# The head of a two-layer mixer kernel: x and base_w landing in turn, and sums taken off TensorE

## The chip, the cores and the metric

One core of one Trainium2 chip. The metric is the device time of one execution of the kernel, in microseconds (us), taken as the median of several runs. The engines are named as in the profile: PE is TensorE, ACT is ScalarE, DVE is VectorE, POOL is GpSimd, SP is the engine whose queue issues most DMAs. PE works on SBUF operands and writes PSUM banks (`ps`, 8 banks of 128 x 512 float32).

## The reference

Two layers, each with a small conditioning part and a mixture-of-experts part, on x of 64 x 32 x 512. Cut to what matters:

```
def _L0_cond_ref(x, embedding, W0, b0, W1, b1, W2, b2, weight, bias_k):
    h = jax.nn.gelu(embedding @ W0 + b0, approximate=False)
    h = jax.nn.gelu(h @ W1 + b1, approximate=False)
    att = jax.nn.softmax((h @ W2 + b2) / T, axis=-1)
    agg_w = jnp.einsum('bk,koi->boi', att, weight[..., 0])
    agg_b = att @ bias_k
    return jnp.einsum('boi,bih->boh', agg_w, x) + agg_b[:, :, None]

def _L0_ffn_ref(x, gate_w, base_w, base_b, lora_A, lora_B):   # E=8, top 2, R=16
    gate_logits = jnp.einsum('bsd,ed->bse', x, gate_w)
    weights, selected = jax.lax.top_k(gate_logits, K)
    weights = jax.nn.softmax(weights, axis=2)
    result = jnp.einsum('bsd,od->bso', x, base_w) + base_b
    w_full = jnp.sum(jax.nn.one_hot(selected, E) * weights[..., None], axis=2)
    low = jnp.einsum('bsd,erd->ebsr', x, lora_A)
    return result + SCALING * jnp.einsum('ebsr,eor,bse->bso', low, lora_B, w_full)

x = x + _L0_ffn_ref(_L0_cond_ref(x, cond_128, ...), ...)
x = x + _L1_ffn_ref(_L1_cond_ref(x, cond_128, ...), ...)
```

`_L1_cond_ref` is a grouped convolution of 9 taps plus a context row per batch, and `_L1_ffn_ref` again a mixture (4 experts, top 2, R=16) without a base product.

## The kernel before, in words

The 2048 rows (64 batches x 32 channels) are cut into G = 4 groups of TG = 4 tiles of 128 rows. The width D = 512 is cut into DC = 4 chunks of 128, and x is held transposed: `xT_s[:, g % 2, c, :]` is chunk c of group g, 128 x 512. Mixing over channels (`agg_w`) commutes with the products over D, so the kernel first multiplies x by the weights and then mixes the small results with `mixT`, a block-diagonal matrix per tile.

Precision: large products are made from parts. A value is split into a high part (float32r, by ACT) and a low part (full minus high, by DVE or POOL), and `hi_lo` (L951 to 958) issues three matmuls: high x high (L955), low x high (L956), high x low (L957).

For group 0 the head does, in PE's program: filler matmuls on a matrix of ones (`keep_busy`, L948); the attention network (L1168 to L1177); the column sums of `lgw` (LoRA A and gate weights together, 136 columns) by a matmul with ones (L1180), which multiply the bias of the mixing; the logits of x by `lgw` in full float32 (`x_logits`, L969, which the compiler splits into two passes); the attention turned and spread over tiles (L1185, L1188); `mixb` and `ctx` (L1193, L1195), which DVE copies out as `mixbias` and `ctxbias`; the product with base_w (`x_base`, into the four PSUM banks `P0`, one per tile); the mixing of the logits (`mix_logits`, L986); the sums of base_w over its inputs (L1209, by ones, and L1217, which turns the row into a column); and the turning of the gated LoRA values (`turn_lw`, L1029). Then comes the first product of group 1 (`x_first(1, t)`, 264 columns, into the same banks `P0`, so it waits for `p0_out(0, t)`, ACT's copy of bank t to SBUF), then `make_y(0)`, four steps of `mix_base` (L1047) and `experts0`, with the bias row (L1058) in the first, then `mix_logits(1)`, the sums for the second layer (L1230), `x_base(1)`, `turn_lw(1)`, the bias row of group 1 and `make_y(1)`. DVE makes `bias_x(i, c)` (x plus bias times the sum of base_w, L717) and `make_x1(i, c)` (L723) from each y; step c >= 2 of `make_y` writes the PSUM bank of step c - 2 and waits for its `make_x1`. From i = 1 on a loop overlaps the second layer of one group with the first layer of a later one.

The order on each engine is the order in which the code is written; semaphores order the engines among each other. All loads go through SP's queue in program order, except `wrep`, which ACT issues. DVE's routing (`route0`) hands `dif` to ACT (`gate_exp`, L465) and takes it back; its result is `lw`. POOL makes the low parts of group 1 (`x_low(1, c)`, tile `xTl`) after `lb_lo`, the low part of LoRA B that DVE makes behind the routing.

## Time and profile before

| | |
|---|---|
| median of 3 runs | 182.52 us (182.43 to 183.62) |
| profiled execution | 182.84 us, of which the span is 181.1 us |
| busy in the span: PE, PE weight load | 174.1 us, 162.4 us |
| busy in the span: DVE, ACT, POOL | 131.9 us, 82.1 us, 84.1 us |
| matmul instructions recorded | 1123 |
| HBM read, written | 7.77 MB, 4.19 MB |

The span runs from the first to the last instruction. Busy times are sums of recorded durations. A matmul's recorded duration includes its way through the array, so that a row of matmuls overlaps; what one costs in a full queue is the distance between starts, which the chain gives.

### The profile page before, as it was taken

The numbers are of one execution on the slowest core, as the hardware profiler recorded it, in microseconds if no ns is written. First come the engines' busy times: TensorE is split into PE (matmuls) and PEld (weight loads), VectorE is DVE, ScalarE is ACT, GpSimd is POOL, SyncE is SP. The second block draws the span as 40 slices with busy tenths as digits, with TensorE's granted clock in tenths as the row PEclk, the third lists the DMA queues.
The fourth block names the chain that finished last, engine by engine and source line by source line (L and its number), as shares of the span: only waits on it lengthen the run. The fifth ranks groups of instructions, "written<-read, shape, count | busy, mean of one in ns | idle before, by whom it ended". The sixth has DMA issues, their size and how long they took to land.

```text
span 181.1 us, 3129 instructions
## 1 busy us (share of the span) xinstructions
PE 174.1 (96%) x1123; PEld 162.4 (90%) x1123; DVE 131.9 (73%) x270; ACT 82.1 (45%) x189; POOL 84.1 (46%) x86
## 2 busy tenths in 40 slices
PE   7999999999999999999999999999999999989990
PEld 7998888988997799999989999999899999988870
DVE  6159999979967943997996436997997943578471
ACT  3657747860635357525143267422315553244021
POOL 7024605992083979950009199630008693434000
PEclk9999999999999999999999999999999999999999
DMA  5999000004200330000033000000131000000336
GB/s 183 304 370 375 25 0 2 0 5 160 72 0 4 125 109 0 4 0 0 2 117 119 0 0 4 0 0 0 43 134 58 2 5 0 0 0 4 116 116 232
DMA packets 6351, 12.16 MB, mean 67 GB/s; under 512 B 704, under 2 KB 1088, under 8 KB 6336
## 3 DMA queue, kind: packets, MB, share of 16 engines
q1 hardware_dynamic: 6192, 11.84, 18.4%
q8 instruction: 9, 0.15, 0.3%
q10 hardware_dynamic: 144, 0.13, 0.3%
q14 instruction: 6, 0.05, 0.1%
HBM read 7.77 MB, written 4.19 MB: 66 GB/s over the span
## 4 chain that ended last, share of the span: by engine, by line
PE 90%; DVE 6%; issue 1%; ACT 0%; POOL 0%; DVEq 0%; POOLq 0%
PE ps L955 22%; PE ps L957 22%; PE ps L956 22%; PE ps L1047 7%; PE ps L948 3%; PE ps L969 2%; PE ps L986 2%; PE ps L1148 2%; PE ps L1149 2%; PE ps L1029 1%; PE ps L1180 1%; PE ps L1209 1%; PE ps L1058 1%; DVE xsl L668 1%; DVE xT_s L717 1%
## 5 line engine op out<-in xcount | busy, mean ns | idle before, releaser
L955 PE MATMUL ps<-xw_h,xTh 128*128 128x264 f32 (+1 forms) x96 | 30.4, 317 | 0.0
L956 PE MATMUL ps<-xw_l,xTh 128*128 128x264 f32 (+1 forms) x96 | 29.9, 311 | 0.0
L957 PE MATMUL ps<-xw_h,xTl 128*128 128x264 f32 (+1 forms) x96 | 29.8, 311 | 0.0
L337 POOL TENSOR_TENSOR xTl<-xT_s,xTh 128x512 fp32r<-128x512 f32 x12 | 15.2, 1299 | 24.1 <-ACT xTh L422 16.9
L736 DVE TENSOR_TENSOR outb<-ps,s_sb 128x340 f32<-128x340 f32 x16 | 8.2, 511 | 16.3 <-PE ps L957 11.9
L353 POOL TENSOR_TENSOR x1Tl<-x1T,x1Th 128x512 fp32r<-128x512 f32 x12 | 16.0, 1345 | 8.5 <-DVE lw L696 8.5
L342 POOL TENSOR_TENSOR zl<-outb,zh 128x340 fp32r<-128x340 f32 x15 | 14.4, 962 | 10.5 <-ACT zh L457 10.4
L1047 PEld LDWEIGHTS ps<-mixT,xp 128*128 128x128 f32 x128 | 16.4, 191 | 2.3 <-DVE x1T L723 1.1
L956 PEld LDWEIGHTS ps<-xw_l,xTh 128*128 128x128 f32 x96 | 18.1, 188 | 0.1
L955 PEld LDWEIGHTS ps<-xw_h,xTh 128*128 128x128 f32 x96 | 18.1, 188 | 0.1
L957 PEld LDWEIGHTS ps<-xw_h,xTl 128*128 128x128 f32 x96 | 18.1, 188 | 0.0
L1047 PE MATMUL ps<-mixT,xp 128*128 128x128 f32 x128 | 17.2, 277 | 0.3 <-DVE x1T L723 0.3
L457 ACT ACTIVATE zh<-outb 128x340 fp32r<-128x340 f32 x16 | 7.8, 489 | 17.4 <-DVE outb L736 12.7
L723 DVE SCALAR_TENSOR_TENSOR x1T<-ps,side_s,xT_s 128x512 f32<-128x512 f32 x16 | 12.0, 748 | 4.2 <-PE ps L957 3.6
L353 POOL TENSOR_TENSOR xTl<-x1T,xTh 128x512 fp32r<-128x512 f32 x4 | 6.0, 1502 | 16.9 <-ACT xTh L480 16.8
L717 DVE SCALAR_TENSOR_TENSOR xT_s<-ps,sum_w,xT_s 128x512 f32<-128x512 f32 x16 | 11.7, 744 | 1.9 <-PE ps L1058 1.9
L445 ACT ACTIVATE xp<-ps 128x384 f32<-128x384 f32 x12 | 5.9, 490 | 14.3 <-PE ps L957 14.2
L346 POOL TENSOR_TENSOR zl<-outb,zh 128x272 fp32r<-128x272 f32 x15 | 12.0, 799 | 0.0
L777 DVE TENSOR_TENSOR xs<-x1T 128x256 f32<-128x256 f32 x12 | 10.7, 910 | 0.6
L465 ACT ACTIVATE ex<-dif 128x32 f32<-128x32 f32 (+1 forms) x8 | 1.8, 221 | 20.6 <-DVE dif L651 20.6
L451 ACT ACTIVATE s_sb<-ps 128x340 f32<-128x340 f32 x16 | 7.1, 443 | 8.5 <-PE ps L957 8.4
L955 PE MATMUL ps<-zh,tap_h 128*128 128x272 f32 x36 | 10.5, 291 | 0.2 <-DVE zl L668 0.2
...
## 6 DMA issues: line engine op xcount, KB each, us to landing
xT_s<-in_xT_dram SPq DMA_DIRECT2D x16, 256.0 KB, 4.5
out_dram<-outb SPq DMA_DIRECT2D x16, 256.0 KB, 2.3
x1T<-in_wT_dram SPq DMA_DIRECT2D x4, 256.0 KB, 6.1
...
x1T<-in_lbT_dram SPq DMA_DIRECT2D x1, 256.0 KB, 8.0
outb<-in_b1T_dram SPq DMA_DIRECT2D x1, 256.0 KB, 9.4
```

Of the source, the lines that this page charges most:

```text
L337: nc.gpsimd.tensor_tensor(lo[:, c, :], xT_s[:, g % 2, c, :], hi[:, c, :].bitcast(F32), ALU.subtract).then_inc(x_lo, 1)
L342: nc.gpsimd.tensor_tensor(zl[:, t, 0:QE, :].rearrange("p k e -> p (k e)"), zf[:, t % 2, 0:NE], zh[:, t, 0:QE, :].bitcast(F32).rearrange("p ...
L346: nc.gpsimd.tensor_tensor(zl[:, t, QE:TAPS, :].rearrange("p k e -> p (k e)"), zf[:, t % 2, NE:NE + NO], zh[:, t, QE:TAPS, :].bitcast(F32). ...
L353: nc.gpsimd.tensor_tensor(lo, full, hi.bitcast(F32), ALU.subtract).then_inc(x1_lo, 1)
L717: nc.vector.scalar_tensor_tensor(out=xT_s[:, i % 2, c, :], in0=ps[:, BROW[i], :], scalar=sum_w[:, c:c + 1], in1=xT_s[:, i % 2, c, :], op0= ...
L723: nc.vector.scalar_tensor_tensor(out=x1T[:, i % 2, c, :], in0=ps[:, Y[c], :], scalar=side_s[:, S_BB + c:S_BB + c + 1], in1=xT_s[:, i % 2, ...
L736: nc.vector.tensor_tensor(zf[:, t % 2, 0:NE], ps[:, ring(t, "U"), 0:NE], s_sb[:, t % 2, :], ALU.add).then_inc(ze_ok, 1)
L777: nc.vector.tensor_tensor(full, even, odd, ALU.add).then_inc(xs_ok, 1)
L955: nc.tensor.matmul(dst, sh, mh, start=start and c == 0, stop=False)
L956: nc.tensor.matmul(dst, sh, ml, start=False, stop=False)
L957: last = nc.tensor.matmul(dst, sl, mh, start=False, stop=stop and c == n - 1)
L1047: nc.tensor.matmul(ps[:, Y[c], cols(t)], p0[:, t, cols(c)], mixer(i, t), start=t == 0, stop=False)
```

## The change: what it does

It rearranges the first 60 us of the program and takes some sums off PE:

- The loads of x (group 0) and base_w (`wT`) alternate by chunk. A second copy of base_w, by rows (`wrow`, from the host), is loaded into the SBUF place of `p0`, after the first mix sum (`agg_ok`), ahead of `tapw` and `b1T`.
- `x_logits` goes by chunk of D instead of by tile, and `x_base` of chunks 0 and 1 stands between the chunks. Eight of the filler matmuls in the attention network become four, and two more behind L1180 go.
- The sum of `lgw` over chunks is first made by two additions on POOL, so that one matmul remains of four (two instructions of eight), behind the logits. The same for the second layer's sums (`az_t`).
- The sums of base_w by PE (L1209, L1217) and their copies go. ACT reads each of the four row chunks of `wrow` with a Copy that also gives the sum (`accum_out`), ahead of the four `p0_out`.
- `ud` gets its own place. DVE's and ACT's orders are changed to fit, and in group 1 the bias row stands two tiles earlier, with `bias_x(1, c)` and `sums_high` moved forward.

```diff
+        ud = sb("ud", [P, 2, NO])
+
+        wrow_s = p0
+
+        lgw_t = lw[:, :, :].rearrange("p t e -> p (t e)")[:, 0:3 * LG].rearrange("p (c e) -> p c e", c=3)
+        az_t = sb("az_t", [P, 3, PJ])
...
                 load_xT(0, c)
+                sp.dma_start(wT_s[:, c, :], wT[:, c, :]).then_inc(in_base[c], 16)
             sp.dma_start(side_s[:, :], side).then_inc(in_side, 16)
-            for c in range(DC):
-                sp.dma_start(wT_s[:, c, :], wT[:, c, :]).then_inc(in_base[c], 16)
             sp.dma_start(az_s, az).then_inc(in_az, 16)
             sp.dma_start(lbT_s, lbT).then_inc(in_lb, 16)
             for c in range(DC):
                 load_xT(1, c)
+            sp.wait_ge(agg_ok, 1)
+            for c in range(DC):
+                sp.dma_start(wrow_s[:, c, :], wrow[:, c, :]).then_inc(in_wrow[c], 16)
             sp.dma_start(tapw_s, tapw).then_inc(in_tap, 16)
...
+            pool.wait_ge(in_lgw, 16)
+            nc.gpsimd.tensor_tensor(lgw_t[:, 0:2, :], lgw_s[:, 0:2, :], lgw_s[:, 2:4, :], ALU.add).then_inc(const_step, 1)
+            pool.wait_ge(const_step, 3)
+            nc.gpsimd.tensor_tensor(lgw_t[:, 2, :], lgw_t[:, 0, :], lgw_t[:, 1, :], ALU.add).then_inc(lgt_ok, 1)
             pool.wait_ge(in_early, 16)
             pool.wait_ge(attT_ok, 1)
             bias_rows(0)
             pool.wait_ge(in_az, 16)
             nc.gpsimd.tensor_tensor(ue[:, :, :], az_s[:, 0, :, :], az_s[:, 1, :, :], ALU.subtract).then_inc(dif_ok, 1)
+            nc.gpsimd.tensor_tensor(az_t[:, 0:2, :], az_s[:, 0, :, 2 * PJ:3 * PJ], az_s[:, 1, :, 2 * PJ:3 * PJ],
+                                    ALU.add).then_inc(const_step, 1)
+            pool.wait_ge(const_step, 4)
+            nc.gpsimd.tensor_tensor(az_t[:, 2, :], az_t[:, 0, :], az_t[:, 1, :], ALU.add).then_inc(azt_ok, 1)
             pool.wait_ge(base_lo, DC)
-            pool.wait_ge(base_hi, DC)
-            nc.gpsimd.tensor_tensor(ud, az_s[:, 0, :, PJ:NE], az_s[:, 1, :, 0:NO], ALU.subtract).then_inc(dif_ok, 1)
+            x_low(1, 0)
+            x_low(1, 1)
+            pool.wait_ge(lb_lo, 1)
+            x_low(1, 2)
+            x_low(1, 3)
+            nc.gpsimd.tensor_tensor(ud[:, :, :], az_s[:, 0, :, PJ:NE], az_s[:, 1, :, 0:NO], ALU.subtract).then_inc(dif_ok, 1)
             shifted_low(1, sw_l[:, :, :], az_s[:, 1, :, :], sw_h[:, :, :])
...
             x_high(0, 0)
-            x_high(0, 1)
+            base_high(0)
             act.wait_ge(attT_mm, 1)
             nc.scalar.activation(attT[:, :], attT_b, ACT.Copy).then_inc(attT_ok, 1)
-            x_high(0, 2)
-            x_high(0, 3)
-            base_high(0)
+            for c in range(1, DC):
+                x_high(0, c)
+                base_high(c)
+            act.wait_ge(zero_ok, 1)
+            mix_place(0)
+            xl_out(0)
+            xl_out(1)
+            nc.scalar.activation(xw_h[:, :, 0:LG], lgw_s[:, :, :], ACT.Copy).then_inc(lgw_hi, 1)
+            act.wait_ge(in_az, 16)
+            nc.scalar.activation(sw_h[:, :, :], az_s[:, 1, :, :], ACT.Copy).then_inc(suv_hi, 1)
+            x_high(1, 0)
+            x_high(1, 1)
             act.wait_ge(lgsum_mm, 1)
             nc.scalar.activation(lg_sum[:, :], ps[:, LGS, 0:LG], ACT.Copy).then_inc(lgsum_ok, 1)
-            base_high(1)
-            xl_out(0)
-            base_high(2)
-            base_high(3)
-            xl_out(1)
-            nc.scalar.activation(xw_h[:, :, 0:LG], lgw_s[:, :, :], ACT.Copy).then_inc(lgw_hi, 1)
-            act.wait_ge(zero_ok, 1)
-            mix_place(0)
-            act.wait_ge(in_az, 16)
-            nc.scalar.activation(sw_h[:, :, :], az_s[:, 1, :, :], ACT.Copy).then_inc(suv_hi, 1)
             act.wait_ge(zero_ok, 2)
             bias_high(0)
+            gate_exp(0, gate0, dif0_ok, ex0_ok)
+            act.wait_ge(in_lb, 16)
+            nc.scalar.activation(lb_h[:, :], lbT_s, ACT.Copy).then_inc(lb_hi, 1)
+            x_high(1, 2)
+            x_high(1, 3)
             act.wait_ge(dif_ok, 1)
             nc.scalar.activation(uw_h[:, :, :], ue[:, :, :], ACT.Copy).then_inc(suv_hi, 1)
-            act.wait_ge(in_lb, 16)
-            nc.scalar.activation(lb_h[:, :], lbT_s, ACT.Copy).then_inc(lb_hi, 1)
-            act.wait_ge(dif_ok, 2)
-            nc.scalar.activation(vw_h[:, :, :], ud, ACT.Copy).then_inc(suv_hi, 1)
-            gate_exp(0, gate0, dif0_ok, ex0_ok)
-            act.wait_ge(bsum_mm, 1)
-            nc.scalar.activation(row_w[:, :], ps[0:1, BSUM, :], ACT.Copy).then_inc(bsum_ok, 1)
             for c in range(DC):
-                x_high(1, c)
+                act.wait_ge(in_wrow[c], 16)
+                nc.scalar.activation(wrow_s[:, c, :], wrow_s[:, c, :], ACT.Copy,
+                                     accum_out=sum_w[:, c:c + 1]).then_inc(wsum_ok, 1)
+            act.wait_ge(wsum_ok, DC)
             for t in range(TG):
                 p0_out(0, t)
...
+            act.wait_ge(dif_ok, 2)
+            nc.scalar.activation(vw_h[:, :, :], ud[:, :, :], ACT.Copy).then_inc(suv_hi, 1)
...
+            sums_high(0, 0)
+            sums_high(0, 1)
             p0_out(1, 2)
             lwT_high(1)
             p0_out(1, 3)
-            for t in range(TG):
-                sums_high(0, t)
+            sums_high(0, 2)
+            sums_high(0, 3)
...
-            for c in range(DC):
-                x_low(c)
+            x_low(0)
             base_low(0)
+            x_low(1)
+            base_low(1)
             dve.wait_ge(attb_mm, 1)
             dve.wait_ge(in_wrep, 16)
             mix_sum(1, prods[0], 0, TG)
-            base_low(1)
-            base_low(2)
-            base_low(3)
...
+            x_low(2)
+            base_low(2)
+            x_low(3)
+            base_low(3)
...
-            dve.wait_ge(wsum_mm, 1)
-            nc.vector.tensor_copy(sum_w[:, :], ps[:, WSUM, 0:DC]).then_inc(wsum_ok, 1)
...
             sums(0, 0)
             sums(0, 1)
+            bias_x(1, 0)
             lwT_low(1)
-            bias_x(1, 0)
             sums_low(0, 0)
             sums(0, 2)
+            bias_x(1, 1)
             sums_low(0, 1)
             sums(0, 3)
             make_x1(1, 0)
             sums_low(0, 2)
             sums_low(0, 3)
-            for c in range(1, DC):
-                bias_x(1, c)
-                make_x1(1, c)
+            make_x1(1, 1)
+            bias_x(1, 2)
+            make_x1(1, 2)
+            bias_x(1, 3)
+            make_x1(1, 3)
...
-            def x_logits(half, tiles=(0, 1)):
+            def x_logits(c):
                 pe.wait_ge(in_lgw, 16)
-                for t in (2 * half + a for a in tiles):
-                    for c in range(DC):
-                        pe.wait_ge(xT_in[0][c], 16)
-                        last = nc.tensor.matmul(ps[:, XLG[half], lg_cols(t)], xT_s[:, 0, c, cols(t)], lgw_s[:, c, :],
-                                                start=c == 0, stop=c == DC - 1)
-                if tiles[-1]:
-                    last.then_inc(xl_mm, 1)
+                pe.wait_ge(xT_in[0][c], 16)
+                for t in range(TG):
+                    last = nc.tensor.matmul(ps[:, XLG[t // 2], lg_cols(t)], xT_s[:, 0, c, cols(t)], lgw_s[:, c, :],
+                                            start=c + t % 2 == 0, stop=c == DC - 1 and t % 2 == 1)
+                    if c == DC - 1 and t % 2:
+                        last.then_inc(xl_mm, 1)
...
-            keep_busy(4, 4)
+            keep_busy(4, 2)
             pe.wait_ge(h1_ok, 1)
             nc.tensor.matmul(ps[:, HID, 0:NB], early_s[:, A_W1:A_W1 + P], h1T[:, :], start=True, stop=True).then_inc(h2_mm, 1)
             pe.wait_ge(consts, 3)
             nc.tensor.matmul(ps[0:NB, ATT, 0:K0], ones[0:1, 0:NB], early_s[0:1, A_B2:A_B2 + K0], start=True, stop=False)
-            keep_busy(4, 4)
+            keep_busy(4, 2)
             pe.wait_ge(h2_ok, 1)
             nc.tensor.matmul(ps[0:NB, ATT, 0:K0], h2T[:, :], early_s[:, A_W2:A_W2 + K0], start=False, stop=True).then_inc(att_mm, 1)
-            pe.wait_ge(in_lgw, 16)
-            for c in range(DC):
-                last = nc.tensor.matmul(ps[:, LGS, 0:LG], ones[:, :], lgw_s[:, c, :], start=c == 0, stop=c == DC - 1)
-            last.then_inc(lgsum_mm, 1)
-            keep_busy(4, 2)
-            x_logits(0, (0,))
+            x_logits(0)
             pe.wait_ge(att_ok, 1)
             nc.tensor.transpose(attT_b, att_n[:, :], ident[0:NB, 0:NB]).then_inc(attT_mm, 1)
             pe.wait_ge(place_ok, 1)
             pe.wait_ge(att_ok, 2)
             nc.tensor.matmul(attb_b, place_r[:, :, :].rearrange("b j c -> b (j c)"),
                              att_d[:, :, :].rearrange("b t k -> b (t k)"), start=True, stop=True).then_inc(attb_mm, 1)
-            x_logits(0, (1,))
             x_logits(1)
+            for t in range(TG):
+                x_base(0, t, (0,))
             pe.wait_ge(attT_ok, 1)
             nc.tensor.matmul(mixb_b, early_s[0:K0, A_MB:A_MB + P], attT[:, :], start=True, stop=True).then_inc(mixb_mm, 1)
             pe.wait_ge(in_side, 16)
             nc.tensor.matmul(ctx_b, side_s[:, S_CTX:S_CTX + P], early_s[:, A_COND:A_COND + NB],
                              start=True, stop=True).then_inc(ctx_mm, 1)
-            pe.wait_ge(lgsum_ok, 1)
-            for t in range(TG):
-                x_base(0, t, (0,))
+            x_logits(2)
+            x_logits(3)
             for t in range(TG):
                 x_base(0, t, (1,))
+            pe.wait_ge(xl_ok, 2)
+            pe.wait_ge(lgt_ok, 1)
+            nc.tensor.matmul(ps[:, LGS, 0:LG], ones[:, :], lgw_t[:, 2, :], start=True, stop=True).then_inc(lgsum_mm, 1)
             pe.wait_ge(mixb_ok, 1)
             pe.wait_ge(ctx_ok, 1)
             for t in range(TG):
                 mix_logits(0, t)
-            pe.wait_ge(base_lo, DC)
-            for n, part in enumerate((base_h, base_l)):
-                for c in range(DC):
-                    last = nc.tensor.matmul(ps[:, BSUM, :], ones_r[:, :], part[:, c, :],
-                                            start=n + c == 0, stop=n == 1 and c == DC - 1)
-            last.then_inc(bsum_mm, 1)
             for c in range(2, DC):
                 for t in range(TG):
                     x_base(0, t, (c,))
-            pe.wait_ge(bsum_ok, 1)
-            for c in range(DC):
-                last = nc.tensor.matmul(ps[:, WSUM, c:c + 1], row_w[0:1, cols(c)], ones[0:1, 0:1], start=True, stop=True)
-            last.then_inc(wsum_mm, 1)
             turn_lw(0)
             for c in range(DC):
                 for t in range(TG):
@@ -1223,19 +1232,15 @@
             make_y(0)
             for t in range(TG):
                 mix_logits(1, t)
-            pe.wait_ge(in_az, 16)
+            pe.wait_ge(azt_ok, 1)
             pe.wait_ge(x1_ok, DC)
-            for m in range(2):
-                for h in range(2):
-                    last = nc.tensor.matmul(psum_b, ones[:, :], az_s[:, m, h, 2 * PJ:3 * PJ],
-                                            start=m + h == 0, stop=m + h == 2)
-            last.then_inc(pjsum_mm, 1)
+            nc.tensor.matmul(psum_b, ones[:, :], az_t[:, 2, :], start=True, stop=True).then_inc(pjsum_mm, 1)
             x_base(1, 0)
             x_base(1, 1)
+            bias_row(1)
             x_base(1, 2)
             turn_lw(1)
             x_base(1, 3)
-            bias_row(1)
```

How the instructions stand. PE, from the end of the attention network to the first products with base_w, before (L1180 are the sums over `lgw`, L969 the logits, L955 to L957 `x_base`):

```order
L1177 MATMUL ps<-early_s,h2T 64x8
L1180 MATMUL ps<-lgw_s,ones 128x136 x4
L948 MATMUL ps<-ones_r 128x256 x2
L969 MATMUL ps<-lgw_s,xT_s 128x136 x4
L1185 MATMUL ps<-ident,att_n 8x64
L1188 MATMUL ps<-att_d,place_r 128x128
L969 MATMUL ps<-lgw_s,xT_s 128x136 x12
L1193 MATMUL ps<-attT,early_s 128x64
L1195 MATMUL ps<-early_s,side_s 128x64
L955 MATMUL ps<-xw_h,x1Th 128x512
```

and now (L990 are the logits, L977 to L979 `x_base`, L1210 and L1212 `mixb` and `ctx`):

```order
L1198 MATMUL ps<-early_s,h2T 64x8
L990 MATMUL ps<-lgw_s,xT_s 128x136 x4
L1201 MATMUL ps<-ident,att_n 8x64
L1204 MATMUL ps<-att_d,place_r 128x128
L990 MATMUL ps<-lgw_s,xT_s 128x136 x4
L977 MATMUL ps<-xw_h,x1Th 128x512
...
L1210 MATMUL ps<-attT,early_s 128x64
L1212 MATMUL ps<-early_s,side_s 128x64
L990 MATMUL ps<-lgw_s,xT_s 128x136 x8
L977 MATMUL ps<-xw_h,x1Th 128x512
```

The sums over `lgw` have left this place, and `x_base` of chunk 0 stands ahead of `mixb` and `ctx`.

ACT, from the first gate's Exp (L465) to the turned LoRA values (L469), before:

```order
L465 ACTIVATE ex<-dif 128x32
L549 ACTIVATE row_w<-ps 1x512
L422 ACTIVATE xTh<-xT_s 128x512 x4
L443 ACTIVATE xp<-ps 128x512 x4
L469 ACTIVATE lwTh<-ps 128x512
```

and now (L565 are the row sums, L459 the four `p0_out`):

```order
L481 ACTIVATE ex<-dif 128x32
L558 ACTIVATE lb_h<-x1T 128x512
L438 ACTIVATE xTh<-xT_s 128x512 x2
L562 ACTIVATE uw_h<-s_sb 128x680
L565 ACTIVATE xp,sum_w<-xp 128x512 x4
L459 ACTIVATE xp<-ps 128x512 x4
L485 ACTIVATE lwTh<-ps 128x512
```

Four row sums, `lb_h` and `uw_h` have come between the Exp and the `p0_out`; two `x_high` of group 1 and the copy of the row have left.

DVE, from the first mix sum (L672, L676) to the logits step (L688), before:

```order
L672 TENSOR_TENSOR xp<-ps,wrep_s 128x4x256
L676 TENSOR_REDUCE late<-xp 128x128
L668 TENSOR_TENSOR xw_l<-x1T,xw_h 128x512 x3
L823 COPY mixbias<-ps 32x16 x4
L828 TENSOR_SCALAR ctxbias<-ps,side_s 32x16 x4
L668 TENSOR_TENSOR xw_l<-lgw_s,xw_h 128x4x136
L688 SCALAR_TENSOR_TENSOR xp<-lg_sum,mixbias,ps 128x136 x4
```

and now:

```order
L692 TENSOR_TENSOR xp<-ps,wrep_s 128x4x256
L696 TENSOR_REDUCE late<-xp 128x128
L841 COPY mixbias<-ps 32x16 x4
L846 TENSOR_SCALAR ctxbias<-ps,side_s 32x16 x4
L688 TENSOR_TENSOR x1Tl<-xT_s,x1Th 128x512
L688 TENSOR_TENSOR xw_l<-x1T,xw_h 128x512
L688 TENSOR_TENSOR x1Tl<-xT_s,x1Th 128x512
L688 TENSOR_TENSOR xw_l<-x1T,xw_h 128x512
L688 TENSOR_TENSOR xw_l<-lgw_s,xw_h 128x4x136
L708 SCALAR_TENSOR_TENSOR xp<-lg_sum,mixbias,ps 128x136 x4
```

The low parts of chunks 2 and 3 have moved behind the copies of `mixbias` and `ctxbias`.

## Rows read from the trace of the kernel before

**Rows 1.** The page, 40 equal slices of the span: busy tenths of PE, and granted clock.

```profile
PE   7999999999999999999999999999999999989990
...
PEclk9999999999999999999999999999999999999999
```

**Rows 2.** The chain that ended last, 0 to 63 us: start us, us, what.

```profile
1.24 2.93 PE ps L948 x12
...
7.68 2.11 PE ps L1180 x8
...
11.80 2.98 PE ps L969 x24
...
22.05 1.85 PE ps L1209 x8
...
23.91 0.24 PE ps L955
...
29.45 0.98 PE ps L1217 x8
30.43 0.59 PE ps L1029 x4
...
36.89 0.89 PE ps L1047 x8
...
44.99 0.89 PE ps L1230 x8
...
54.83 0.44 PE ps L1058
...
60.67 1.16 PE ps L1047 x8
...
62.29 0.24 PE ps L957
```

**Rows 3.** DMA: x's issues of groups 0 and 1; then the page's row of base_w.

```profile
L270 SPq DMA_DIRECT2D xT_s<-in_xT_dram x8: 424/438/607, 1.7 to 9.3; - x8
...
DMA to landing us min/median/max: 5.3/7.0/8.3
...
x1T<-in_wT_dram SPq DMA_DIRECT2D x4, 256.0 KB, 6.1
```

**Rows 4.** ACT in order of time: start us, us, engine, line, operation.

```profile
8.07 0.19 ACT L518 ACTIVATION_READ_ACCUMULATOR att_e<-ps,att_m 64x1 f32 x1
...
19.73 0.75 ACT L542 ACTIVATE uw_h<-s_sb 128x680 fp32r<-128x680 f32 x1
...
24.95 0.23 ACT L465 ACTIVATE ex<-dif 128x32 f32<-128x32 f32 x1 [3.40 <-DVE dif L651]
...
25.57 2.18 ACT L422 ACTIVATE xTh<-xT_s 128x512 fp32r<-128x512 f32 x4
...
27.65 2.44 ACT L443 ACTIVATE xp<-ps 128x512 f32<-128x512 f32 x4
```

**Rows 5.** DVE in order of time.

```profile
17.03 1.89 DVE L668 TENSOR_TENSOR xw_l<-x1T,xw_h 128x512 fp32r<-128x512 f32 x3
...
18.83 0.71 DVE L823 COPY mixbias<-ps 32x16 f32<-32x16 f32 x4
...
20.57 1.97 DVE L668 TENSOR_TENSOR xw_l<-lgw_s,xw_h 128x544 fp32r<-128x544 f32 x1
...
22.58 1.16 DVE L688 SCALAR_TENSOR_TENSOR xp<-lg_sum,mixbias,ps 128x136 f32<-128x136 f32 x4
...
26.89 0.69 DVE L696 TENSOR_TENSOR lw<-xp,w 128x512 f32<-128x512 f32 x1
...
28.94 1.22 DVE L672 TENSOR_TENSOR x1T<-ps,wrep_s 128x1024 f32<-128x1024 f32 x1
...
36.98 0.69 DVE L676 TENSOR_REDUCE late<-above 128x64 f32<-128x512 f32 x1
```

**Rows 6.** POOL in order of time.

```profile
20.33 1.63 POOL L357 TENSOR_TENSOR sw_l<-x1T,sw_h 128x680 fp32r<-128x680 f32 x1
...
29.10 5.03 POOL L337 TENSOR_TENSOR xTl<-xT_s,xTh 128x512 fp32r<-128x512 f32 x4 [7.14 <-DVE lb_l L668]
```

24 lines of the change are left out of this document (10 added, 14 removed).

## The prediction

> **What bounds the kernel now.** I read the slices of the page first [rows 1]: TensorE (PE) is at nine tenths or more in nearly every slice from the second to the thirty-ninth, and its granted clock reads full, which is the higher of its two levels (2.4 GHz). So I went to the chain that ended last [rows 2]: up to 62 us it is matmuls, but for one knot of VectorE (DVE) work at 55 to 61. A microsecond of matmuls taken out of this head is a microsecond gained, as long as the other engines deliver that much earlier. Whether they do is the question, and it is read from the DMA landings [rows 3] and the timelines of ScalarE (ACT), DVE and GpSimd (POOL) [rows 4 to 6]. After the head PE stays at nine in the slices, so what the head gains should arrive at the end: I carry it over one for one.
>
> One thing on pace. The twelve filler matmuls of 256 columns at the start take 0.244 us each; those of `x_base`, with 512 columns, later take 0.231 (5.54 us for the 24 between 23.91 and 29.45) [rows 2]. So the first ones run at half the later pace though the clock is shown as granted. The sums over `lgw` (L1180) still take 0.264 each; the 24 logits matmuls of the same 136 columns from 11.80 take 0.124 [rows 2]. The pace doubles between them, near 10 us.
>
> **What goes from PE.** L1180 keeps 2 of 8 instructions and moves behind the logits, where one costs 0.124: 2.11 - 0.25 = 1.86 us less. L1209 goes: 1.85. L1217 goes: 0.98. L1230 keeps 2 of 8: 0.67 less [rows 2]. That is 5.4 us. Six fillers of 0.244 go too, up to 1.5 us; what they are worth the walk below tells, since they fill waits. If PE alone counted, the time would fall by over 6 us.
>
> **PE walked through the new order.** With two fillers less the second layer starts when `h1T` is there, some 0.4 earlier; the next two give 0.6 more: the attention logits end near 6.6 instead of 7.68 [rows 2]. The first chunk of x lands at 1.72 + 5.3 = 7.0 [rows 3], so PE waits 0.4 there. Then, at half pace until 10: logits of chunk 0, 8 x 0.264, to 9.2; the two attention matmuls, 0.4, to 9.6; logits of chunk 1, two slow and six fast, to 10.9. `x_base` of chunk 0, 12 x 0.231, to 13.7; the `mixb` and `ctx` matmuls, 0.7, to 14.4; logits of chunks 2 and 3, 16 x 0.124, to 16.4; `x_base` of chunk 1 to 19.2; the `lgw` sum to 19.4; `mix_logits`, 8 x 0.124, to 20.4; `x_base` of chunks 2 and 3, 5.54, to 25.9; `turn_lw`, 0.59, to 26.5 against 31.0 before. DMA doesn't bind this: a chunk takes 5.3 to 6.1 from issue to landing [rows 3], and SP issues one each half microsecond, so the last chunk of x, issued near 5.1, lands near 11.1 and is wanted at 14.4; the last of base_w comes near 12.
>
> **DVE in that time.** Its first mix sum is done by 14, and `mixbias` waits for `ctx` at 14.4; the eight small copies take 1.7 [rows 5], to 16.2. The four subtractions that now stand behind them (x and base_w, chunks 2 and 3) take 0.63 each, to 18.7. Then the low part of `lgw`. In the trace it took 1.97 us, where subtractions of like size take 0.63 [rows 5], and POOL's `sw_l` ran from 20.33 to 21.96 beside it [rows 6]; DVE finished 0.6 after POOL. In the new order POOL may start an `xTl` (1.26 each [rows 6]) just when DVE starts this one. Either DVE waits for it, and the logits step starts at 20.7, or DVE is first, and it starts at 20.1, when `lg_sum` and the first `mix_logits` are there. I take 20.7, the nearer row. The Trainium skill, GPSIMD Engine Reference, section Specifications, says that GpSimd's SBUF interfaces are shared with VectorE, with contention for DVE instructions that have two SBUF inputs; by it the first case holds, and the trace agrees with 1.97 against 0.63.
>
> From the logits step it took 2.4 us to `gate_exp` (22.58 to 24.95) and 5.0 to the end of `lw` (27.58) [rows 4, 5]: 23.1 and 25.7. PE wants `lw` at 25.9, so `turn_lw` just fits.
>
> **ACT, where the stall moves.** Behind `gate_exp(0)` in ACT's queue now stand `lb_h` and two `x_high` (0.545 each, from 2.18 for four), `uw_h` (0.75 long, 0.68 of the queue) and the four row sums, and only then the four `p0_out`. A row sum is a copy of 512 columns, 0.545, and a read of the accumulator. The only such read in the trace is 0.19 long, behind an Exp, and the next instruction starts 0.09 after it [rows 4]: a sum costs 0.64 to 0.73, I take 0.68, so 2.7 for four. From 23.2 that makes 25.6 for the start of the first sum and 28.2 for the first `p0_out`, done at 28.8; the fourth is done at 30.4. Before, they ran from 27.65 to 30.09 and nobody waited [rows 4]. Now `x_first(1, 0)` waits from 26.5 to 28.8, and later tiles are fed 0.55 apart where PE needs 0.37. Chunk 0 ends near 30.7, and chunks 1 to 3 (36 x 0.122, from 5.87 for 48 between 31.02 and 36.89 [rows 2]) at 35.1. Before: 36.89. **Of 4.5 us of lead PE keeps 1.8**; the rest stands in front of ACT. The copy of base_w by rows is not what is late: it is issued after the first mix sum, near 14.2, behind transfers that ended at 9.3 + 8.3 = 17.6 [rows 3], and ACT asks for it at 25.6. POOL's last two `xTl` wait for `lb_lo`, near 27.1, are done by 29.7, and are wanted from 32.
>
> DVE is next in line: its mix sums and the low part of `lw` took 8.7 us, from 28.94 to 37.67 [rows 5]; from 27.1 that is 35.9, and `bias_x(0, 0)` can start at 36.4, when the bias row's matmul ends. ACT's stall covers it, by half a microsecond.
>
> **After 35.** `make_y(0)` keeps its length. L1230 gives 0.67. Then the knot: DVE made `bias_x(1, 0)` only after `bias_row(1)`, which ended at 55.26, and PE's L1047 waited for DVE at 60.67: `make_y(1)` took 7.27 (55.26 to 62.53), where a step of L1047 and three matmuls costs 0.89 + 0.70 = 1.6, four 6.4 [rows 2]. With the bias row two tiles earlier DVE has `bias_x` of two chunks behind it when the first y is ready. That can give all 0.87; but DVE's sums then run beside POOL's `x1Tl`, as the `lgw` step did, and it may be only 0.3. I take 0.55.
>
> **Sum:** 1.8 + 0.67 + 0.55 = 3.0 us. The profiled execution took 182.84 (span 181.1) and would take 179.8. It lies 0.3 above the median of the runs, 182.52, so **I predict 179.5 us**.
>
> **Rivals.**
> A. Nothing waits for ACT: row sums cheap, the gate 2 us earlier. Then PE goes from 26.5 through `x_first` to 32.4, and DVE's mix sums, done at 35.9, are the wall: y of chunk 2 starts near 37.4, and `make_y(0)` ends near 40.6 instead of 42.1. A gain of 4.5: 178.0. For it speaks only that DVE may be ahead in its collision with POOL (0.6). Chance 0.07.
> B. ACT is later: a row sum at 0.80 (copy 0.61 long and read 0.19 long, one after the other) is 0.5, and as much again by a late gate: a gain of 2.0, 180.5. Chance 0.13.
> C. The pace doubles later than 10 us. PE was never idle from 1.24 to there [rows 2]; now it has fewer fillers, a hole at 6.6 and small matmuls. If the pace comes 3.4 later (10 to 13.4 at half pace), PE is 1.7 late at `ctx`, and DVE, the gate and ACT hang on that in a row: 181.2. The Trainium skill, TensorE: Matmul & The Clock Gate, section What's actually happening, says that the default state is throttled and that activity releases it, a rule that speaks against taking fillers away; the trace agrees in so far as the early matmuls are slow, and not in its clock slices, which read full. Chance 0.15.
> D. Slower than before: the new hole in front of `x_first(1, 0)`, 2.3 us of idle PE and three short ones where the trace has none, costs the pace. The 36 matmuls of chunks 1 to 3 at half pace cost 4.4 more: 179.5 + 4.4 = 183.9. It decides from 25 such matmuls on (3.0 / 0.122). Against it: the hole is short beside the busy stretches around it, and the clock slices never fall. Chance 0.06.
> E. The lead is given back later by something that is not moved: 182.3. Against it the slices of PE [rows 1]. Chance 0.04.
>
> **Chances.** The forecast 0.55 (179.0 to 180.3). A measurement of this kernel tells about 1% from no change, 180.7 to 184.3. Faster: forecast, A and half of B, 0.69. Same: the other half of B, C, E and part of D, 0.26. Slower: 0.05, the rest of D and whatever is worse. The range takes in A, B and C: 178.0 to 181.5.
>
> **What would show it.** Right: the logits of chunk 0 start near 7.0; `mixbias` at 14.4; `turn_lw` near 26; the row sums from 25.6 for 2.7 us; PE idle for 2 us before its first 264-column matmul, with `p0_out` named; the first L1047 near 35.1; `make_y(1)` without long waits for DVE; all later rows 3.0 earlier. Wrong: slow matmuls after 10 us, row sums above 0.8 each or waiting for their DMA, `turn_lw` waiting for `lw`, or a lead at 62 us that is not there at the end.

## The result: slower, where faster was forecast

The changed kernel took 184.11 us (median of 22 runs, 182.28 to 185.81), the kernel before 182.45 on the same chip (22 runs, 181.08 to 184.52): a ratio of 1.0098, with a 95% interval of 1.0075 to 1.012. The ratios here are formed from those executions of either kernel that took no more than 1.5% longer than its fastest, and so are not quite the quotients of the medians. The forecast was 179.5. The profiled execution of the changed kernel took 184.52, with a span of 182.8. It lost PE's full clock twice, as the slices of its page show, where the clock in [rows 1] has nines throughout:

```profile
PE   7889995999999999999999999999999999989990
...
PEclk9958999699999999999999999999999999999999
```

The slices are 4.6 us wide. The stretches show it closer (us from and to, length, busy us of PE, PEld, DVE, ACT, POOL with their instructions, granted clock, DMA share, GB/s):

```profile
6.00:8.00 2.00, 1.52 (x12) 1.18 (x10) 0.56 (x4) 1.99 (x4) 0.00 (x0) 1.00 0.99 210
...
8.00:9.00 1.00, 0.84 (x4) 0.49 (x3) 1.00 (x3) 0.79 (x3) 0.02 (x1) 0.73 0.99 272
9.00:10.00 1.00, 0.11 (x2) 0.09 (x1) 0.45 (x1) 0.17 (x1) 1.00 (x1) 0.50 0.95 297
...
10.00:14.00 4.00, 4.00 (x13) 3.56 (x14) 3.38 (x4) 2.99 (x5) 0.35 (x1) 0.50 1.02 347
14.00:16.00 2.00, 2.00 (x7) 1.56 (x6) 0.37 (x1) 1.62 (x5) 0.00 (x0) 0.68 1.02 397
16.00:20.00 4.00, 4.00 (x27) 3.42 (x26) 2.62 (x10) 1.43 (x4) 2.38 (x3) 1.00 1.05 392
...
28.00:30.00 2.00, 0.95 (x7) 0.58 (x5) 1.94 (x4) 2.00 (x7) 0.47 (x1) 1.00 0.00 0
30.00:32.00 2.00, 1.03 (x7) 0.89 (x7) 1.93 (x3) 1.97 (x6) 2.00 (x2) 1.00 0.00 0
32.00:34.00 2.00, 2.00 (x11) 1.93 (x11) 1.97 (x4) 2.00 (x4) 2.00 (x3) 0.59 0.00 0
34.00:36.00 2.00, 2.00 (x12) 2.00 (x12) 1.90 (x4) 1.93 (x6) 2.00 (x2) 0.56 0.00 0
```

A clock of 0.50 is the lower level, 1.2 GHz, and 1.00 the upper, 2.4 GHz. The first fall came at 8.5: the clock was still 0.97 from 8.0 to 8.5, and 0.50 from there on. It followed, 1.7 us later, a wait of 0.47 us for the first chunk of x that ended at 6.84. The longer wait, 0.89 for the second chunk, began only at 9.06, when the clock was already down. The second fall, near 32.4, stands behind stretches in which PE was busy half the time: 0.95 and 1.03 of 2.00 at 28 to 32. While the clock is low PE counts as fully busy; "busy" doesn't tell slow from fast. The chain that ended last names the waits (start us, us, what); it answers to [rows 2]:

```profile
2.66 7.15 DMA xT_s<-in_xT_dram
9.95 2.15 PE ps L990 x8
12.10 0.43 PE ps L977
...
15.70 0.24 PE ps L977
...
16.76 0.36 PE ps L1212 x2
...
27.84 2.46 ACT xp L565 x8
30.32 0.61 ACT xp L459
30.97 0.39 PE ps L977
...
38.96 0.89 PE ps L1068 x8
```

The second chunk of x landed at 2.66 + 7.15 = 9.81; `x_base` then cost 0.43 a matmul instead of 0.23; and at 28 the chain leaves PE for ACT's row sums (L565) and the first `p0_out` (L459). The base-and-mix step begins at 38.96. Before, it began at 36.89 [rows 2]: 2.07 later here, and the span is 1.7 longer. So what was lost was lost before 39 us. ACT's and PE's timelines at that hole (start, us, engine, line, operation; in brackets the idle time before it and what ended it), beside [rows 4]:

```profile
25.39 0.23 ACT L481 ACTIVATE ex<-dif 128x32 f32<-128x32 f32 x1 [2.51 <-DVE dif L671]
...
27.75 0.62 ACT L565 ACTIVATE xp<-xp 128x512 f32<-128x512 f32 x1
28.27 0.18 ACT L565 ACTIVATION_READ_ACCUMULATOR xp<-xp 128x1 f32 x1
28.36 0.61 ACT L565 ACTIVATE xp<-xp 128x512 f32<-128x512 f32 x1
...
30.97 0.39 PE L977 MATMUL ps<-xw_h,xTh 128*128 128x264 f32 x1 [2.02 <-ACT xp L459]
31.20 0.28 PE L978 MATMUL ps<-xw_l,xTh 128*128 128x264 f32 x1
...
33.48 0.42 PE L978 MATMUL ps<-xw_l,xTh 128*128 128x264 f32 x1
```

From one row sum to the next it is 0.61. PE waited 2.02 us, ran ten matmuls at 0.12 from start to start (0.23 for the first of each three), and then some fifteen at 0.22.

### The profile page after: what moved, and what is told of

It is laid out like the page before. It is cut to its first block, busy times and chain, and to the rows that moved or that the text cites. A ratio compares the mean times of both kernels' runs of the same rounds, so it can differ in the third digit from the quotient of the medians.

```text
span 182.8 us, 3076 instructions
## 1 busy us (share of the span) xinstructions
PE 172.2 (94%) x1089; PEld 159.7 (87%) x1089; DVE 130.3 (71%) x269; ACT 84.8 (46%) x196; POOL 86.3 (47%) x90
## 4 chain that ended last, share of the span: by engine, by line
PE 72%; DVE 14%; ACT 4%; DMA 4%; issue 3%; SPq 1%; DVEq 0%; ACTq 0%
PE ps L977 19%; PE ps L978 18%; PE ps L979 18%; PE ps L1068 7%; DMA xT_s<-in_xT_dram 4%; DVE xs L797 4%; PE ps L990 2%; PE ps L1169 2%; PE ps L1007 2%; PE ps L1170 2%; ACT xp L565 1%; DVE xsl L688 1%; DVE rank L676 1%; DVE outb L785 1%; ACT xsh L501 1%
## 5 line engine op out<-in xcount | busy, mean ns | idle before, releaser
L977 PE MATMUL ps<-xw_h,xTh 128*128 128x264 f32 (+1 forms) x96 | 31.6, 329 | 2.0 <-ACT xp L459 2.0
L978 PE MATMUL ps<-xw_l,xTh 128*128 128x264 f32 (+1 forms) x96 | 30.5, 318 | 0.0
L979 PE MATMUL ps<-xw_h,xTl 128*128 128x264 f32 (+1 forms) x96 | 30.5, 318 | 0.0
L344 POOL TENSOR_TENSOR xTl<-xT_s,xTh 128x512 fp32r<-128x512 f32 x12 | 15.7, 1335 | 24.5 <-ACT xTh L438 16.7
L977 PEld LDWEIGHTS ps<-xw_h,xTh 128*128 128x128 f32 x96 | 18.8, 195 | 2.8 <-ACT xp L459 2.3
L978 PEld LDWEIGHTS ps<-xw_l,xTh 128*128 128x128 f32 x96 | 18.8, 196 | 0.1
L979 PEld LDWEIGHTS ps<-xw_h,xTl 128*128 128x128 f32 x96 | 18.8, 196 | 0.0
L1068 PE MATMUL ps<-mixT,xp 128*128 128x128 f32 x128 | 17.1, 276 | 0.3 <-DVE x1T L743 0.3
L797 DVE TENSOR_TENSOR xs<-x1T 128x256 f32<-128x256 f32 x12 | 12.8, 1088 | 0.6
L977 PE MATMUL ps<-zh,tap_h 128*128 128x272 f32 x36 | 10.5, 291 | 0.2 <-DVE zl L688 0.2
```

What stands on the lines that cost most here:

```text
L344: nc.gpsimd.tensor_tensor(lo[:, c, :], xT_s[:, g % 2, c, :], hi[:, c, :].bitcast(F32), ALU.subtract).then_inc(x_lo, 1)
L797: nc.vector.tensor_tensor(full, even, odd, ALU.add).then_inc(xs_ok, 1)
L977: nc.tensor.matmul(dst, sh, mh, start=start and c == 0, stop=False)
L978: nc.tensor.matmul(dst, sh, ml, start=False, stop=False)
L979: last = nc.tensor.matmul(dst, sl, mh, start=False, stop=stop and c == n - 1)
L1068: nc.tensor.matmul(ps[:, Y[c], cols(t)], p0[:, t, cols(c)], mixer(i, t), start=t == 0, stop=False)
```

## Experiments

All ratios are to the kernel before, on the same chip and with a 95% interval; times of steps are from each kernel's profiled execution. e1 to e6 and e8 to e10 are edits of the changed kernel, e7 and e11 of the kernel before.

**e1: fillers back in the head.** Two calls of `keep_busy(4, 2)` become `(4, 4)` again, and three stand anew:

```diff
+            keep_busy(4, 2)
             x_logits(0)
...
+            keep_busy(4, 6)
             x_logits(1)
+            keep_busy(4, 2)
             for t in range(TG):
                 x_base(0, t, (0,))
```

> The changed kernel with filler matmuls put back in the head: both pairs are four again, two stand before the logits of chunk 0, six before those of chunk 1 (where PE waited 0.9 us for x) and two behind them. Theory P (pace): holes in PE's work at 6.4 and 8.9 us cost the fast pace, shown by the granted clock at 0.5 from 8.7 to 15.4 us. It expects a granted clock of 1.00 there, the logits of chunk 1 and x_base of chunk 0 done about 2.6 us earlier (8 x 0.13 and 7 x 0.20), ctx near 14.6 instead of 17.1, and 182.0 us in all instead of 184.1. Rival L (late engines): the head is late because its loads land later, whatever the pace; PE then waits elsewhere, and the time stays at 184.1 within 0.7.

183.67 us, ratio 1.0094 (1.0063 to 1.0125). The clock stayed at 1.00 up to 29.5 us, `x_base` cost 0.23 from 11.2 on, and `ctx` was done at 14.9 instead of 17.1. (That the fillers kept the clock isn't shown by this one profile: in e4 below, which leaves the head as the change has it, the clock stayed at 1.00 too, and `ctx` was done at 14.97.) Yet the time is that of the changed kernel, as the rival said. The row sums began at 27.0, 0.84 earlier than there and not 2.2, so most of the gain had gone before ACT. DVE and POOL show where:

```profile
15.75 0.97 DVE L846 TENSOR_SCALAR ctxbias<-ps,side_s 32x16 f32<-32x16 f32 x4
16.75 1.65 DVE L688 TENSOR_TENSOR x1Tl<-xT_s,x1Th 128x512 fp32r<-128x512 f32 x1
18.31 0.97 DVE L688 TENSOR_TENSOR xw_l<-x1T,xw_h 128x512 fp32r<-128x512 f32 x1
...
22.65 1.31 DVE L669 TENSOR_TENSOR eq<-xp 128x256 f32<-128x256 f32 x1
...
16.19 1.66 POOL L376 TENSOR_TENSOR s_sb<-x1T 128x680 f32<-128x680 f32 x1 [5.38 <-DMA x1T<-in_az_dram]
17.80 0.93 POOL L377 TENSOR_TENSOR az_t<-x1T 128x136 f32<-128x136 f32 x1
...
20.70 2.97 POOL L344 TENSOR_TENSOR xTl<-xT_s,xTh 128x512 fp32r<-128x512 f32 x2 [1.23 <-DVE xw_l L688]
```

DVE's subtractions of 0.69 took 1.65 and 0.97, and its first compare 1.31, each beside a POOL instruction. In the changed kernel DVE came to its subtractions at 18.98, behind POOL's: 0.69 each. PE, itself 2 us early, waited 0.96 for `lw` and then 2.23 for `p0_out` (from 28 to 30 it was busy 0.00 of 2.00), and the clock fell to 0.50 before that wait had ended. An earlier PE met a DVE that wasn't, and the hole became longer. The clock is not the whole of the loss: two of e1's eight executions had a mean clock of 0.999, and they took 183.66 and 183.68, no less than the others.

**e2: the hole filled.** Sixteen fillers between `turn_lw(0)` and `x_first`:

```diff
             turn_lw(0)
+            pe.wait_ge(lgsum_ok, 1)
+            keep_busy(1, 16)
```

> The changed kernel with 16 fillers between turn_lw(0) and x_first(1, 0), where PE idled 2.0 us and the granted clock then fell to 0.5 from 32.7 to 35.9 us. Theory P: the fall goes, the 15 or so matmuls of 264 columns at 0.22 us take 0.12, 1.5 us less, 182.6 us. Rival L: the fall comes from the hole's sum with the next row of waits and not from idleness, or DVE's mix sums (done at 38.1) bound the place anyway: the first L1068 comes no more than 0.9 earlier, 183.2 or more.

182.74 us, ratio 1.0031 (1.0003 to 1.006). The first stretch below is that in which the fillers run; the clock doesn't fall behind it:

```profile
28.00:30.00 2.00, 2.00 (x17) 1.87 (x17) 1.97 (x3) 1.97 (x8) 0.91 (x1) 1.00 0.00 0
30.00:32.00 2.00, 2.00 (x16) 1.79 (x15) 1.93 (x3) 2.00 (x5) 2.00 (x3) 1.00 0.00 0
32.00:34.00 2.00, 2.00 (x18) 2.00 (x17) 1.97 (x4) 2.00 (x4) 2.00 (x2) 1.00 0.00 0
```

`x_first` began at 30.62, 0.35 earlier than without fillers, and the base-and-mix step at 37.06, 1.90 earlier; between them lie 6.4 us instead of 8.0. Nothing but useless matmuls was added. The head was left as it is, and its clock fell there too, to 0.59 in the stretch from 16 to 20, this time behind a wait of 1.42 for the load of side.

**e3: both fillings.**

> The change as it is, with the fillers of e1 in the head and the sixteen fillers of e2 ahead of x_first together, so that no pace is lost and the order of ACT stays late. Theory: the row sums on ACT still hold p0_out to 30.1 as in e1, x_first then runs at full pace to 36, DVE's wall at 36.9 stands behind: the first tile of the base-and-mix step at 36.5 to 37 where e2 had 37.06: 182.3, ratio 1.002 (1.000 to 1.004). Rival (the two add): e1 gave 0.4 and e2 1.4, so 182.1 less another 0.8: 181.3, ratio 0.997.

182.24 us, ratio 1.0028 (1.0002 to 1.0055). The base-and-mix step began at 36.21. With the clock at 1.00 up to there, the change is just no faster than the kernel before: the wait for ACT is still there, filled.

**e4: row sums early.** The only edit is that the four row sums stand ahead of the gate's Exp on ACT:

```diff
+            for c in range(DC):
+                act.wait_ge(in_wrow[c], 16)
+                nc.scalar.activation(wrow_s[:, c, :], wrow_s[:, c, :], ACT.Copy,
+                                     accum_out=sum_w[:, c:c + 1]).then_inc(wsum_ok, 1)
             gate_exp(0, gate0, dif0_ok, ex0_ok)
...
-            for c in range(DC):
-                act.wait_ge(in_wrow[c], 16)
-                nc.scalar.activation(wrow_s[:, c, :], wrow_s[:, c, :], ACT.Copy,
-                                     accum_out=sum_w[:, c:c + 1]).then_inc(wsum_ok, 1)
```

> The changed kernel with ACT's four row sums moved ahead of gate_exp(0), into the 2.5 us in which ACT waited for dif; nothing else. Theory Q (queue order): the sums are 2.44 us in front of p0_out, so x_first starts at 28.9 (behind turn_lw) instead of 31.0, 2.0 less; and with the hole gone theory P adds the pace, 1.5 more: 180.6 us. Q without P: 182.1. Rival: the copy by rows lands too late for that place (it landed at 20.3 to 22.3), or DVE's mix sums, done at 38.1, become the bound: the first L1068 at 37.6 at the earliest, 182.7 us.

181.06 us, ratio 0.9952 (0.9928 to 0.9977): 1.5% less than the changed kernel's ratio, and the first version that is faster than the kernel before. ACT did the sums from 20.62 to 23.17, while it would have waited for DVE (in the changed kernel 2.51 idle before the Exp). PE's clock stayed whole behind 28, and the base-and-mix step began at 34.1, 4.9 earlier. Not all of that is the edit's: the head, which it doesn't touch, had kept its clock in this execution, and the Exp came 0.75 earlier. Over all executions the edit is worth the 1.5%. In the base-and-mix step the next wall stood:

```profile
38.93 1.16 PE L1068 MATMUL ps<-mixT,xp 128*128 128x128 f32 x8 [1.03 <-DVE x1T L743]
```

DVE had no idle time from 28.6 to 37.3: five mix products, their sums, and the low part of `lw`.

**e5: the old order of loads.**

```diff
                 load_xT(0, c)
-                sp.dma_start(wT_s[:, c, :], wT[:, c, :]).then_inc(in_base[c], 16)
             sp.dma_start(side_s[:, :], side).then_inc(in_side, 16)
+            for c in range(DC):
+                sp.dma_start(wT_s[:, c, :], wT[:, c, :]).then_inc(in_base[c], 16)
```

> The changed kernel with the loads in the order of before: four chunks of x, side, four of base_w; nothing else. Theory M (alternating loads land late by themselves: chunk 1 of x took 7.15 us from issue, and the core moved 111 and 156 GB/s at 5 to 7 us where it moved 260 and 293 before): it expects those rates back, x chunk 1 landed at 7.7, logits of chunk 1 at 8.7, and x_base of chunk 0 waiting for base_w, landed at 9.9, until 11.2; ctx near 15.0, 182.5 us. Rival: the low rate at 5 to 7 us is the chip's and varies from run to run, so the order changes nothing, or the later base_w makes it slower: 184.1 to 185.5.

183.32 us, ratio 1.0086 (1.0051 to 1.0121), no better. x was there sooner, but `x_base` of chunk 0 now waited 2.65 for the low part of base_w, and the clock was at 0.72 from 10 to 14 and at 0.50 from 14 to 18. The alternate order isn't what costs. In this execution it was again a wait of PE in the sparse head, and the clock fell before that wait had ended.

e5 shows one thing more. ACT's order is the changed kernel's, and PE waited as long as there for `p0_out`, 2.04 us, till 32.85. But here the clock stayed:

```profile
30.00:32.00 2.00, 0.80 (x6) 0.47 (x4) 1.97 (x3) 2.00 (x8) 0.59 (x1) 1.00 0.00 0
32.00:34.00 2.00, 1.15 (x7) 1.01 (x8) 1.93 (x3) 1.97 (x6) 2.00 (x3) 1.00 0.00 0
34.00:37.00 3.00, 3.00 (x25) 2.93 (x26) 2.93 (x5) 3.00 (x6) 3.00 (x3) 1.00 0.00 0
```

`x_first` took 6.5 us (32.85 to 39.37) and not 8.0. So a hole of 2 us can cost the pace, and need not.

**e6, e8, e9: more on top of e4.** e6 adds e1's fillers; e8 loads side behind the first chunk of x and of base_w instead of behind all eight transfers, since `ctx` had waited for it in e4; e9 is both. The edit of e8:

```diff
                 sp.dma_start(wT_s[:, c, :], wT[:, c, :]).then_inc(in_base[c], 16)
+                if c == 0:
+                    sp.dma_start(side_s[:, :], side).then_inc(in_side, 16)
-            sp.dma_start(side_s[:, :], side).then_inc(in_side, 16)
```

> The row sums ahead of the gate as in e4, and the fillers of the old head as in e1 together. My theory now: in e4 DVE ends the walk between 27 and 37 us (its mix sums from 28.62 to 37.4 with no idle time), so a head that is earlier by the fillers is worth only what it brings forward in DVE. The gate's first compare in e1 stood at 22.73 and in e4 at 22.82, so the fillers bring DVE 0.1 forward: 180.9 us, ratio to before 0.994 to 0.998, the same as e4. Rival (PE's pace in the head is what counts): x_base of chunk 0 starts earlier by a microsecond and the end with it: 180.0 us, ratio 0.990.

> The row sums early as in e4, and the load of side placed behind the first two chunks instead of behind all eight, since in e4 the ctx matmul waited for it till 14.54 and the logits of chunk 2 stood behind. Theory: DVE binds from 20 on, and DVE's mixbias waits for ctx at 14.5; with side there by 9, ctx runs at about 12.8, DVE's queue is a microsecond earlier up to the gate, and the end with it unless POOL's x1 parts hold it: 180.2 us, ratio 0.991. Rival (the order of loads doesn't matter, the sixteen DMA queues are full): side takes the place of x chunk 1, everything is as late as before: 181.0, ratio 0.995.

> Row sums early, fillers of the old head, side early, together. Theory: DVE binds, so it gets what e8 gets and no more: 180.2 us, ratio 0.991. Rival (the fillers keep PE's pace where the other two leave short waits, and each part adds): 179.5 us, ratio 0.987.

180.77, 180.85 and 180.88 us; ratios 0.9947 (0.9915 to 0.9979), 0.994 (0.9914 to 0.9966) and 0.9958 (0.993 to 0.9986). None can be told from e4 or from another. In all three PE waited 1.00 to 1.01 us for DVE at the third chunk of the base-and-mix step. What PE or a load brought forward ended at the same wall. The 180.2 that I had expected of e8 and e9 did not come. Ahead of `turn_lw` PE waited 1.75 us for `lw` in e8 and 1.45 in e9, and the clock stayed at 1.00 behind both. In e8 DVE's low part of base_w took 2.14 and a compare 1.52 beside POOL.

**e7: the later order alone,** in the kernel before: `bias_row(1)` two tiles earlier, and DVE's and ACT's work at that place in the changed kernel's order. On PE:

```diff
             x_base(1, 1)
+            bias_row(1)
             x_base(1, 2)
             turn_lw(1)
             x_base(1, 3)
-            bias_row(1)
```

> The kernel before, with nothing of the change but the later order: bias_row(1) two tiles earlier on PE, the sums of tile 0 and bias_x(1, 1) earlier on ACT and DVE. It measures the term that the prediction put at 0.55 us by itself. By the trace of after the sums on DVE, beside POOL's x1Tl, took 1.86 for two and 1.31 for one, and the knot gave nearly nothing: expected ratio 0.999 (0.997 to 1.001). By the prediction's term: 0.55 us less, 0.997. Rival: the collision costs more than the order gives: 1.002.

182.16 us, ratio 1.0002 (0.9976 to 1.0029). From the first matmul of the base-and-mix step to that of its eighth chunk (the fourth of the second group) it took 23.76 us, and 23.94 before: 0.2 less, which the time doesn't show.

**e10: POOL kept away from DVE.** e8, and POOL begins group 1's first two low parts of x only behind the gate's Exp:

```diff
             pool.wait_ge(base_lo, DC)
+            pool.wait_ge(ex0_ok, 1)
             x_low(1, 0)
             x_low(1, 1)
```

> e8 (row sums early, side early) and one wait more: POOL starts the low parts of x's chunks 0 and 1 of the next group only when the gate's exp is there, so that they do not run beside DVE's low part of lgw and the gate's compares. In e8 those took 0.99 and 1.52 where they are 0.41 to 0.71 without POOL beside them. Theory (DVE is the bound from 20 to 37): 1.2 saved ahead of the gate, some 0.6 given back at lw and lb_l, which then stand beside the two: 180.2, ratio 0.991. Rival (DVE has slack there, or the collision only moves): 180.85 as e8, ratio 0.994 to 0.997.

181.55 us, ratio 0.9961 (0.9935 to 0.9987), where the theory had 180.2; the rival held. The compares took 0.41 and 0.42 again, and two small instructions behind them, beside the same POOL work now at 24.65, rose from 0.19 to 0.66 and 0.78. The collision only moved, onto small instructions.

**e11: a hole in the kernel before.** Nothing of the change; seven idle copies on ACT ahead of its first `p0_out`:

```diff
+            for k in range(7):
+                if k:
+                    act.wait_ge(spare_ok, k)
+                nc.scalar.activation(spare[:, :, :], ones[:, :].unsqueeze(1).to_broadcast([P, DC, P]),
+                                     ACT.Copy).then_inc(spare_ok, 1)
             for t in range(TG):
                 p0_out(0, t)
```

> The kernel before, with nothing of the change, but seven copies of 512 columns on ACT into a spare tile, ahead of its first p0_out, each behind the one before it. It makes in the old, full program the hole that the change made: x_first(1, 0) must wait. At 0.66 each they are 4.6, the first p0_out is done near 32.9 instead of 28.3, and PE, free at 31.0, is idle for about 1.9. Theory (a hole costs PE pace also when what surrounds it is dense): the hole, plus some 15 matmuls of 264 columns at half pace, 1.8: the first L1047 of the base-and-mix step is 3.7 later, at 40.6, of which the knot at 60 gives nothing back: 186 us, ratio 1.020. Rival (the loss in after came from a head that was already sparse; in the old head a hole costs its length): 1.9 and no more, 183.9, ratio 1.010.

185.67 us, ratio 1.021 (1.017 to 1.025), as the theory had it. All six executions had a mean clock of 0.985 to 0.990, where the kernel before has 0.996 to 1.000. PE waited 1.76 us, and behind it the clock fell in a program whose head had been full:

```profile
28.00:30.00 2.00, 2.00 (x14) 1.51 (x12) 1.94 (x4) 1.91 (x4) 1.13 (x1) 1.00 0.00 0
30.00:32.00 2.00, 0.79 (x6) 0.53 (x6) 1.97 (x4) 1.90 (x5) 2.00 (x3) 1.00 0.00 0
32.00:34.00 2.00, 1.45 (x9) 1.30 (x9) 0.62 (x1) 2.00 (x6) 2.00 (x3) 0.97 0.01 4
34.00:36.00 2.00, 2.00 (x11) 1.99 (x10) 1.49 (x3) 2.00 (x4) 2.00 (x2) 0.50 0.00 0
36.00:38.00 2.00, 2.00 (x13) 2.00 (x13) 1.90 (x4) 1.85 (x8) 2.00 (x3) 0.68 0.00 0
```

`x_first` began at 32.55 instead of 31.02 and took 7.95 instead of 5.87 [rows 2], some fourteen of its matmuls at 0.22 instead of 0.12; the base-and-mix step began at 40.50 instead of 36.89. So 3.6 us were lost with a hole of 1.76. Of the 2.1 that `x_first` took longer, some 0.6 is not the clock's: e5, at the full clock, took 6.5, with ACT's four copies coming 0.5 apart, slower than PE takes them.

**e12: the kernel before again,** to see its two groups of times.

> The kernel before itself, for a second profile of it. Its runs fall into two groups, near 181.5 and near 182.7 us, and the profiled execution on which the prediction rests, 182.84, lies in the upper one. If this one falls into the lower group, the trace should show where the 1.2 us are. Theory: the early matmuls leave their half pace about a microsecond sooner (before 9 us instead of near 10), so that the 24 logits matmuls or the ones of lgw start at full pace. Rival: the difference lies behind the head, in the store at the end or in the bodies; then the first matmul of the base-and-mix step stands at 36.9 in both.

182.59 us, and a ratio of 1.0033 (0.9985 to 1.0081) of the kernel to itself; e2 and e3, at 1.0031 and 1.0028, are no further from the kernel before than that. It doesn't settle the question of the groups: the profiled execution took 184.55 and lies above both. It shows only that the kernel before has such a collision too: the difference of `az` came to POOL at 13.61, ahead of DVE's `xw_l` at 14.13 and not behind it (14.36 and 14.04 in the first profile), DVE took 2.11 for 0.68, and the base-and-mix step began 1.3 later.

## Why the prediction was wrong

**What bounds the kernel, and what goes from PE: right.** The matmuls that were to go went. The time fell by none of them, because the walk behind them failed at two steps, each of which I had weighed as a rival and priced too low in chance.

**PE walked through the new order: wrong, by 2.7 us at `ctx`** (14.4 forecast, 17.12 measured). First, "DMA doesn't bind this". I had taken 5.3 to 6.1 from issue to landing; the second chunk of x took 7.15, and PE waited 0.89 for it. That alone is the small part: logits of chunk 1 began at 9.95 instead of 9.6. Second, the pace: it was there at 6.84, earlier than forecast (eight logits in 1.16), and was gone at 8.5, before that wait had begun. So the logits of chunk 1 took 2.15 where 1.3 was forecast, and `x_base` of chunk 0 took 4.3 from 12.10 where 2.8 was forecast. That is rival C's place with another mechanism: the pace didn't come late, it went. It doesn't go in every execution: in e4's, with the same head, it stayed. e1, whose head was on time, shows that this half of the error was worth little by itself. The words "the clock slices never fall", by which I held D unlikely, were true of a trace in which PE never waited, and so said nothing of what a wait does.

**DVE in that time: the mechanism right, its place wrong.** I expected the collision with POOL at the low part of `lgw`; that took 0.72, and the first compare behind it 0.89 instead of 0.41. The logits step began at 22.54 instead of 20.7 and the Exp at 25.39 instead of 23.1. So DVE made up 0.4 of the 2.7. With an earlier PE, as in e1, e4, e6 and e8, the collisions came back at the subtractions: in e1 DVE lost some 2 us that a walk by undisturbed rows leaves out. The Trainium skill, GPSIMD Engine Reference, section Specifications, has the rule that GpSimd contends for its SBUF interfaces with DVE instructions of two SBUF inputs; the runs agree (0.69 becomes 1.65, 0.41 becomes 1.31). In e10 two instructions of 128x32, 0.19 long when alone, took 0.66 and 0.78, which speaks for a wait and not for half speed.

**ACT, where the stall moves: the right place, the sizes near.** A row sum cost 0.61 (forecast 0.68), the four 2.57 with the start of the next (2.7). PE's hole was 2.02 (forecast from 26.5 to 28.8, 2.3), and `x_first` began at 30.97 instead of 28.8, by the head's lateness alone. But I priced the hole at its length and left "the pace" to rival D at 0.06. **This is the step that failed worst.** `x_first` took 8.0 us where 6.3 was forecast: 1.7. In e2, with the hole filled, it took 6.4, and in e5, where the clock stayed through the same hole, 6.5; e11 makes the loss in the kernel before (3.6 for a hole of 1.76). Rival D had named the mechanism. It counted 36 matmuls at half pace, 4.4 us, and 25 as the point from which it decides; some fifteen came, and they were enough because the head was late too. The Trainium skill, TensorE: Matmul & The Clock Gate, section HAM oscillation — how this bites in real kernels, tells of waits for DMA between bursts of matmuls, longer than this hole, that send the clock back every time. Here single holes of 2.02 and 1.76 us (e11) were enough, and one of 2.04 (e5) didn't do it.

**DVE next in line: right.** "ACT's stall covers it" held, and e4 uncovered it: PE waits 1.03 for `x1T`. Rival A's wall stood at the chunk where it was put, at 38.93 against its 37.4, since the Exp came at 24.64 and not at 23.1, from which the end of DVE's mix sums was worked out: 37.3 instead of 35.9.

**After 35: 0.55 measured of 1.2 forecast.** From the first to the eighth chunk of the base-and-mix step it took 23.39 us, before 23.94. All of that had come by the fifth, the first of group 1 (17.84, before 18.45), as the shorter sums of L1230 were to give it (0.67). From there to the eighth it took 5.55, before 5.49: the later order, put at 0.55, gave nothing, and in e7, by itself, 0.2. DVE's sums took 1.86 for two, as before, and then 1.31 for one beside POOL's `x1Tl` (0.43 before), and PE still waited 0.34.

In sum: head late 2.1 us at the first `p0_out` (28.2 forecast, 30.32 measured), `x_first` slow 1.7, and 0.7 less than forecast after 35. That is 4.5 of the 4.7 us between the 179.8 that the profiled execution was to take and the 184.52 that it took. It is the account of one execution, with a mean clock of 0.971; another of the 22 took 184.60 with 0.991. The range, 178.0 to 181.5, did not hold the time, because the two losses came together: one late head made ACT late, and one hole did what D said.

What the change was worth when repaired: e4, with four instructions moved on ACT, 0.9952; with fillers or side early besides, 0.994 to 0.996. Of the 5.4 us of matmuls that it takes from PE, about one shows in the time. In e4's profile PE waits for DVE three times up to 57 us: 0.96 for `lw`, 1.03 and 0.29 for `x1T`.
